# Rotary attention on TensorE: the first two query tiles' scores ahead of the projection unit in two slots of eight

## What is computed

```python
q = apply_rope(split_heads(x @ Wq)); k = apply_rope(split_heads(x @ Wk))
v = split_heads(x @ Wv)
sim = jnp.einsum('bid,bjd->bij', q, k) * scale
sim = jnp.where(causal[None], sim, -jnp.inf)
attn = jax.nn.softmax(sim, axis=-1)
out = jnp.einsum('bij,bjd->bid', attn, v)
return merge_heads(out) @ Wo + bo
```

## Time and profile before

| what | us |
|---|---|
| median of 3 runs (lowest to highest) | 3949.91 (3944.6 to 3952.15) |
| the profiled execution, own time | 3944.43 |
| its span | 3942.7 |
| rotary attention, first to last scores | 1236.6 to 2677.5 |

### The profile page before, as it was taken

One profiled execution on the slowest core, in us unless ns is written; L12 is line 12 of the kernel. 1 busy time (PEld: TensorE's weight loads), 2 busy tenths in 40 slices (PEclk: granted clock), 3 DMA queues, 4 the chain that ended last, 5 costly groups with the idle time before them and its releaser, 6 DMA issues. The chain is left out here.

```text
span 3942.7 us, 89530 instructions
## 1 busy us (share of the span) xinstructions
PE 3455.3 (88%) x30494; PEld 2111.7 (54%) x30494; DVE 2757.4 (70%) x7236; ACT 2286.2 (58%) x5520; POOL 2169.0 (55%) x2263
## 2 busy tenths in 40 slices
PE   5999999985695999999999999995958885987678
PEld 1333333325592566566566566563946774775456
DVE  6888888856454778878888888873437884655565
ACT  2777777763243666666666666662436671864367
POOL 3333333315544777888887888874422332754275
PEclk7999999995697999999999999997979997987879
DMA  5434334413452222222222222222633332110001
GB/s 100 61 59 60 60 60 62 62 17 101 137 193 67 48 55 50 51 56 55 53 57 51 51 57 51 50 55 75 199 92 81 89 82 43 44 45 5 0 1 44
DMA packets 414451, 254.32 MB, mean 65 GB/s; under 512 B 251418, under 2 KB 340434, under 8 KB 412722
## 3 DMA queue, kind: packets, MB, share of 16 engines
q1 hardware_dynamic: 403316, 226.43, 25.0%
q0 software_dynamic: 10688, 22.17, 1.8%
HBM read 91.61 MB, written 45.94 MB: 35 GB/s over the span
## 5 line engine op out<-in xcount | busy, mean ns | idle before, releaser
L2799 POOL TENSOR_TENSOR ra_prob<-ra_prob,ra_inverse 128x256 f32<-128x256 f32 (+3 forms) x512 | 631.1, 1255 | 250.5 <-DVE ra_inverse L3098 249.3
L2577 DVE TENSOR_REDUCE ca_mx<-ca_ps_s 128x2 f32<-128x1024 f32 x512 | 600.6, 1211 | 120.4 <-PE ca_ps_s L2449 120.2
L3012 ACT ACTIVATE ra_prob<-ra_ps_s,ra_low 128x128 f32<-128x128 f32 (+3 forms) x1024 | 533.6, 532 | 228.5 <-DVE ra_low L3078 225.8
L2514 ACT ACTIVATE ca_pT<-ca_ps_p 128x512 f32<-128x512 f32 x1024 | 544.9, 600 | 204.6 <-PE ca_ps_p L2459 203.1
L3078 DVE CUSTOM_DVE_ANT_0 ra_ps_s<-ra_ps_s,ra_mask 128x128 f32<-128x128 f32 (+3 forms) x1024 | 479.9, 510 | 44.1 <-PE ra_ps_s L2954 43.8
L2449 PE MATMUL ca_ps_s<-ca_kst,ca_qst 128*128 128x512 bf16 x1024 | 393.0, 389 | 24.4 <-DMA ca_kst<-ca_bounce 10.9
L2459 PE MATMUL ca_ps_p<-ca_qst,ca_kst 128*128 128x512 bf16 x1024 | 386.7, 383 | 5.5 <-ACT ca_pT L2514 4.2
L3018 ACT COPY ra_probT<-ra_ps_t 128x512 f32<-128x512 f32 x384 | 227.2, 592 | 254.2 <-PE ra_ps_t L2866 254.2
L2866 PE MATMUL ra_ps_t<-ident,ra_prob 128*128 128x128 f32 x2560 | 350.1, 276 | 3.3 <-ACT ra_probT L3018 2.1
L2954 PE MATMUL ra_ps_s<-ra_kz,ra_qz 64*128 64x128 f32 (+3 forms) x2048 | 348.1, 458 | 3.8 <-DMA ra_kz<-ra_rot 2.9
L2792 POOL TENSOR_TENSOR ra_rot<-ra_prod 128x512 f32<-128x512 f32 x256 | 320.6, 1273 | 40.6 <-DVE ra_prod L3087 40.6
(11 more groups left out here) (491 smaller groups left out, 7278.5 us busy)
## 6 DMA issues: line engine op xcount, KB each, us to landing
ra_qz<-ra_rot SPq DMA_DIRECT2D x512, 64.0 KB, 2.0
ra_kz<-ra_rot SPq DMA_DIRECT2D x512, 64.0 KB, 2.0
moe_w_own<-moe_w1T SPq DMA_DIRECT2D x71, 256.0 KB
moe_w_own<-router_w SPq DMA_DIRECT2D x71, 256.0 KB
ca_kst<-ca_bounce SPq DMA_DIRECT2D x256, 64.0 KB
ca_bounce<-ca_thirds SPq DMA_DIRECT2D x192, 64.0 KB
ca_qst<-ca_bounce SPq DMA_DIRECT2D x64, 192.0 KB
moe_hs<-moe_rows SPq DMA_DIRECT2D x71, 66.0 KB, 2.1
```

What stands on the lines that cost most here:

```text
L2514: nc.scalar.activation(pT[:, (NS * hp + u) % PRING, :], ps_p[n % NP][:], ACT.Exp).then_inc(sg["drained"], 1)
L2577: nc.vector.tensor_reduce(mx[:, hm % 2, 2 * j:2 * j + 2], ps_s[m % 2][:].rearrange("p (b k) -> p b k", b=2), AX.X, ALU.max)\
L2799: nc.gpsimd.tensor_tensor(at, at, inverse[:, n % PROB, 2 * tile:2 * tile + 2].unsqueeze(2).broadcast_to([P, 2, keys]), ALU.mult)\
L3012: nc.scalar.activation(prob[:, n % PROB, tile, head, 0:keys], part(n, tile)[:, head, :], ACT.Exp, bias=low[:, n % PROB, at:at + 1], scale= ...
```

## The change

In TensorE's `body`, the call `scores(0, score)` moves from behind the projection (and the other users of `ra_ps_r`) to the head of the slot. It is called in slots 0 and 4 only. No instruction is added or removed, and the text of no other engine changes. Its two waits, `qk_ready` and `exp_done`, move with it and now stand ahead of the waits of `project(0)` and `project(4)`.

```diff
                 def body(j, t, s, front, score, value, out, batch, coming, mixing, routed):
+                    if score is not None and t == 0:
+                        scores(0, score)
                     if front is not None and j < 6:
                         project(j, front)
                     if out is not None and j == 6:
...
                     if routed(RANK) is not None and j == 7:
                         rank(routed(RANK), out)
-                    if score is not None and t == 0:
-                        scores(0, score)
                     if value is not None:
                         for i in fills(t):
                             turn(i, value)
```

## The result

The changed kernel takes 4056.83 us (median of 4 runs, 4052.43 to 4058.69). The kernel before, on the same chip, takes 3948.26 us (3944.6 to 3952.15). That is 108.6 us more, a ratio of 1.0276 (95% interval 1.026 to 1.0292, which is 103 to 115 us). Its profiled execution has a span of 4056.0 us. Within the two profiled executions the stage itself, from the start of the first scores to the start of the last, grew from 1439.7 us (1236.63 to 2676.28) to 1547.9 us (1242.38 to 2790.32), that is by 108.3 us, and the median step from 22.69 to 24.40 us.

What follows compares the result with a forecast made beforehand. The prediction took TensorE's full queue and the chain through DVE, ACT and `ra_ps_r` as both critical. Slot 0 52.5, slot 4 49.9 and start 6.2 gave +108.6 us, so 4058 us, range 4034 to 4080.

Steps and rivals of the forecast that it cites:

- (a): Scores in slots 0 and 4: going ahead gains nothing, because DVE's extrema stand behind its products, which wait for the projection.
- (b): Projection units 0 and 4 go back 0.86 us, so unit 1 gets a new wait of 0.54 us for DVE's products.
- (c): Extrema, exponentials and the values' copy in slot 0 all go back 0.86 us, and unit 2 starts 0.86 us later.
- (d): Slot 4: `project_out` starts 0.86 us later, or 0.66 us in the 13 steps where DVE has other work.
- (e): The scores' wait for landed keys now also holds the projection; no stall was expected, with 1.0 us left.
- (f): Start of the stage: front 1 costs 3.4 us, front 2 1.9 us and its slot 4 0.86 us.
- no change: Rival for the whole kernel: only TensorE's work counts, so a new order is neutral; 3950 us, chance 0.03.
- Half the price: Rival: only the new wait at unit 1 costs, and the values' copy catches up; 4022 us, chance 0.09.
- Faster: Rival: the scores fill a TensorE wait ahead of unit 4 in every step; 3896 us, chance 0.03.
- The rival of a falling clock: Rival: new TensorE gaps lower the granted clock, adding another 73 us over the dense work; 4132 us, chance 0.05.

Runs made afterwards that it cites:

- e3_extrema: The changed kernel with DVE taking the extrema of head 0 ahead of the products in slots 0 and 4; 4017.68 us against 3940.93 for the kernel before.
- e4: The kernel before with only tile 0's scores (a third) put ahead of the projection; 3997.32 us against 3940.93, +56.4 us.
- e5: The kernel before with one extra, unread ACT copy in slots 0 and 4, right behind `fill(0)`; 4005.53 us against 3945.38, +60.1 us.
- e7: The changed kernel with the scores put behind projection and transposes in slots 0 and 4; 4009.95 us against 3947.05 for the kernel before.
- e2_slot4: The kernel before with the scores moved ahead of the projection in slot 4 only; 3990.06 us, +49.1 us.
- e6: The kernel before with one extra, unread ACT copy in slots 0 and 4, ahead of `fill(0)`; 3945.26 us against 3945.38.

## Why the prediction was right

Forecast 4058 us (+108.6 on the profiled execution), measured 4056.83 (+108.6). The firmest check is inside the traces: the profiled executions as wholes are 113.3 us apart, of which 5.75 us arose ahead of the stage, and the stage itself grew by 108.3 us, the step by 1.71 us where 2 x 0.86 was forecast. That the two differences of whole executions agree to the last digit is luck: the interval is 103 to 115 us, and the kernel before came out 1.65 us lower here than the 3949.91 on which the forecast stood. By its parts:

- **(a) no gain from earlier scores.** Confirmed: no reader of the scores starts earlier in the changed kernel. One reading of rows 3 was off: the scores don't end about when the products do but at 1867.52, 0.47 us ahead of them (1867.99), so they had time to spare already. Earlier scores help only if DVE takes the extrema first; e3_extrema is that kernel, and it gets back 32 us of the loss, no more.
- **(b) the wait at unit 1.** 0.54 us forecast, 0.51 shown, because unit 1 starts at S+3.36 and not S+3.38. The distance from scores to projection, which was the unknown size, is 0.85 us where 0.86 was taken.
- **(c) the copy.** Forecast S+5.37 and unit 2 at S+5.44; shown S+5.37 and S+5.43. e3, e4, e5 and e7 each moved one link alone and saw the push pass through. e5 is the strongest, as it touches neither TensorE nor DVE.
- **(d) slot 4.** S+5.63 forecast and shown. The changed kernel has S+5.63 in the steps with DVE's routing work as well, which were at S+4.95 before: 0.68 us, the 0.66 of the sum.
- **(e) keys.** No wait for them in the steady part; e2_slot4 agrees.
- **(f) the start.** The sum of 6.2 us was right by luck, for its terms were not. At the last common place before the first scores the changed kernel's profiled execution is 5.75 us later than that of the kernel before, from earlier stages; this is taken off below. Front 1's slot 0 cost 3.5 us (3.4 forecast). Its slot 4 gave back 0.8 us, which I had put at nothing. Front 2's slot 0 cost 2.6 us (1.9 forecast); the clock fell there, see below. Front 3 started 6.1 us late.

The two errors among the experiments have two causes, and neither stood on the path of the change. In e3_extrema I took the duration of unit 1 or 5 as fixed, and it is 0.10 us longer there. Rows 8 had the sign of it: the unit behind a wait at 1251.12 is 1.13 us long, the one in rows 3 is 1.03. In e7_scores_last I took the end of a row as the moment at which the next instruction of DVE can start, and it starts 0.08 us ahead of it.

The rival "no change" is refuted by the result, and its ground, that only TensorE's own work counts, by e5_copy_behind (+60.1 us with TensorE's instructions as they were). The Trainium skill's page "Perfetto Trace Analysis", section "Identifying the Most-Contended Engine", has one improve the most-contended engine first; in this trace that is TensorE, and its work alone would have given a sum of zero against the 108.6 us measured. "Half the price" had 4022 us, and the wait for the copy that it leaves out is there. "Faster" had 3896, and unit 4 has no wait in the steady part that the scores could fill. The rival of a falling clock is refuted for the steady part: with a wait of 0.51 us at unit 1 or 5 and one of 0.26 to 0.30 us at unit 2 or the output projection, the stretches above have a granted clock of 1.00.

## What to carry to other kernels

When an engine is full, look for the chain that runs beside it and measure, link by link, how far ahead of the instruction that needs it each result arrives, less the time that this instruction takes to start when it does wait. Here the copy ended 0.07 us ahead, a waiting unit started 0.06 us behind it, and so a move of 0.86 us went through to its full size slot after slot. Ask of a reordering who is served later and who is really served earlier: the scores' reader stood in its queue behind the very thing that was put off. The largest wait that a profile shows after a change need not be the one that sets the time, and an extra instruction on a half-idle engine costs all or nothing by its place.

## What the runs showed of the hardware

- The same matmul unit comes in two lengths. Unit 1 or 5 (128x256, four instructions) takes 0.86 to 0.87 us to the next start where its weight load starts 0.11 us ahead of its matmul (kernel before, e4, e5, e6), and 0.96 to 0.97 us where the two start together: behind a wait (the changed kernel, e3) and without one (e7). The extra 0.10 us reached the time where nothing hid it (e3_extrema). That the late load is the cause fits all runs, but none was made to test it, and why it comes late in e7 stays open.
- The granted clock fell once in the middle of the start, after waits of 0.91 and 2.41 us of TensorE close together. Stretches of the changed kernel, columns as in rows 2:

```profile
1256.00:1261.00 5.00, 3.37 (x16) 1.63 (x17) 5.00 (x19) 2.30 (x9) 3.18 (x5) 1.00 0.33 79
1261.00:1266.00 5.00, 1.68 (x10) 0.36 (x6) 4.60 (x13) 4.02 (x14) 5.00 (x4) 1.00 0.38 89
1266.00:1271.00 5.00, 5.00 (x22) 3.46 (x23) 2.45 (x8) 1.07 (x4) 1.07 (x2) 0.66 0.18 44
```

TensorE was busy for 1.68 of 5 us, and in the next 5 us, though it was fully busy, the clock was 0.66 on average, that is, partly at 1.2 GHz and partly at 2.4. From 1268 to 1270 us it was 0.50, the lower level. The same place in the kernel before, with waits of 0.91 and 1.37 us, kept 1.00. So the rival of the clock was a real mechanism. The waits of 0.51 us and less in the steady part left it at 1.00.
